# A decoder in one kernel: buffers re-placed in SBUF so that the matmul operands begin at multiples of 128 bytes

## The reference

```python
x = x + _L0_attn_ref(_layernorm(x), ...)            # 32 heads of 16, 8 kv heads, weights sign(w / s)
x = x + _L0_xattn_ref(_layernorm(x), ctx_4096, ...) # 32 heads of 128, 8 kv heads, q and k RMS-normed
x = x + _L0_ffn_ref(_layernorm(x), ...)             # 1792 wide; of each block of 32 only the argmax row is kept
x = x + _L1_attn_ref(_layernorm(x), ...)            # 32 heads of 16, one kv head, ALiBi, causal
x = x + _L1_xattn_ref(_layernorm(x), ctx_4096, ...) # 32 heads of 16, 8 kv heads, mask
x = x + _L1_ffn_ref(_layernorm(x), ...)             # linear plus 2 of 8 LoRA experts, chosen by a gate
```

## Time and profile before

| | |
|---|---|
| median of 3 runs | 2266.28 us (2264.58 to 2267.7) |
| profiled execution, span from first to last instruction | 2260.1 us |
| median less that span | 6.2 us |
| instructions | 39463 |
| PE busy / weight loads busy | 2193.7 us (97%) / 1735.2 us (77%) |
| VectorE, ScalarE, GpSimd busy | 1368.4, 1016.3, 886.8 us |
| DMA queues' share of 16 engines | 10.1% |
| granted TensorE clock, mean | 0.999 of 2.4 GHz |

### The profile page before, as it was taken

How to read it: one execution, slowest core, us unless ns; L and a number is a source line. 1 busy time by engine, 2 the same in 40 slices (tenths; PEclk the granted TensorE clock), 3 DMA queues, 4 the chain that set the end, 5 groups by cost and what they waited for, 6 DMA issues and landing times. The chain is left out here.

```text
span 2260.1 us, 39463 instructions
## 1 busy us (share of the span) xinstructions
PE 2193.7 (97%) x15918; PEld 1735.2 (77%) x15918; DVE 1368.4 (61%) x2383; ACT 1016.3 (45%) x1734; POOL 886.8 (39%) x659
## 2 busy tenths in 40 slices
PE   7997999999999999999999999999999999999998
PEld 4775878778787787877878777888887777777776
DVE  7887533343333453433333458797785888888866
ACT  6774543445435454344543452111102656666532
POOL 2675231432414413143231345121122768777711
PEclk9999999999999999999999999999999999999999
DMA  4000111110112101011010113000002000100001
GB/s 165 2 20 21 57 38 38 38 57 19 38 38 75 57 20 38 38 38 56 20 38 36 38 54 110 0 0 0 0 1 75 20 1 16 49 26 11 2 1 75
DMA packets 23032, 80.65 MB, mean 36 GB/s; under 512 B 4048, under 2 KB 6224, under 8 KB 16720
## 3 DMA queue, kind: packets, MB, share of 16 engines
q1 hardware_dynamic: 22864, 78.28, 10.1%
HBM read 74.08 MB, written 4.19 MB: 35 GB/s over the span
## 5 line engine op out<-in xcount | busy, mean ns | idle before, releaser
L2566 PE MATMUL xat_TP<-shared_rounded 128*128 128x512 f32 x1024 | 322.6, 396 | 5.8 <-issue 5.8
L2240 POOL TENSOR_TENSOR xat_T<-xat_T,xat_mask 128x512 f32<-128x512 f32 x64 | 81.5, 1296 | 523.5 <-DVE xat_T L2330 523.5
L104 PE MATMUL xat_G<-xat_xnT_hi,shared_rounded 128*128 128x512 f32 x768 | 249.1, 397 | 0.0
L2227 POOL TENSOR_TENSOR shared_rounded<-shared_landing,shared_rounded 128x2048 fp32r<-128x2048 f32 x39 | 179.5, 4612 | 153.2 <-ACT shared_rounded L2084 153.2
L2566 PEld LDWEIGHTS xat_TP<-shared_rounded 128*128 128x128 f32 x1024 | 187.2, 188 | 58.0 <-issue 22.4
L2357 DVE TENSOR_TENSOR X<-X,xat_TP 128x512 f32<-128x512 f32 x128 | 87.0, 680 | 198.4 <-PE xat_TP L2566 198.3
L2321 DVE RECIPROCAL xat_q_inv_rms<-xat_OT 128x16 f32<-128x16 f32 x32 | 8.3, 258 | 322.5 <-PE xat_OT L2493 322.5
L2566 PE MATMUL xat_TP<-shared_rounded,xat_oT_lo 128*128 128x512 f32 x512 | 199.8, 390 | 0.0
L104 PE MATMUL ffn_H<-shared_rounded 128*128 128x448 f32 (+1 forms) x816 | 180.1, 369 | 3.3 <-DVE ffn_h_kept L1394 2.0
L1326 POOL TENSOR_TENSOR ffn_one_hot<-ffn_one_hot,ffn_block_rank 128x448 f32<-128x448 f32 x64 | 75.3, 1177 | 254.5 <-DVE ffn_one_hot L1375 254.5
L684 POOL TENSOR_TENSOR two_T<-two_T,two_row_max 128x512 f32<-128x512 f32 x128 | 131.6, 1050 | 102.5 <-DVE two_row_max L775 102.2
(11 more groups left out here) (362 smaller groups left out, 5024.3 us busy)
## 6 DMA issues: line engine op xcount, KB each, us to landing
shared_landing<-in_Cq_q SPq DMA_DIRECT2D x16, 1024.0 KB, 4.9
shared_landing<-in_Cq_o SPq DMA_DIRECT2D x16, 1024.0 KB, 4.9
shared_landing<-in_Cq_kv SPq DMA_DIRECT2D x8, 1024.0 KB, 6.9
shared_landing<-in_ctxT_paired SPq DMA_DIRECT2D x4, 1024.0 KB, 6.8
two_ctxT_raw<-in_ctxT SPq DMA_DIRECT2D x8, 512.0 KB, 3.7
shared_landing<-in_w1T SPq DMA_DIRECT2D x8, 448.0 KB, 3.9
shared_landing<-in_w SPq DMA_DIRECT2D x7, 512.0 KB, 3.5
out<-X SPq DMA_DIRECT2D x6, 512.0 KB, 3.0
```

Of the source, the lines that this page charges most:

```text
L104: last = eng.matmul(out, a, b, start=(n == 0), stop=(n == len(steps) - 1))
L2227: return eng.tensor_tensor(w[1][:, :, :], landed[:, :, :], w[0][:, :, :].bitcast(F32), ALU.subtract)
L2240: eng.tensor_tensor(T[:, n, :, :], T[:, n, :, :], mask[:, :].unsqueeze(1).to_broadcast([P, ROWS, SEQ]), ALU.add)\
L2566: last = eng.matmul(TP[m % 2][:, :], x, w, start=(n == 0), stop=(n == len(steps) - 1))
```

## The change

No instruction is added, removed or moved on any engine, and no wait changes. Only addresses do: of the 18646 instructions of the built program 350 name another buffer or offset for the layer norm's statistics, on ScalarE, VectorE and GpSimd, and none of these is a matmul.

- The layer norm's 6 x 4 raw statistics (96 bytes) leave `ln_small` and become one buffer `stats` behind `ones`, kept for the whole kernel. `headmask_eps` (32 bytes with its padding) and `stats` (96) together are 128, so the shared buffers get phase 0. `ln_small` shrinks from 160 to 64 bytes.
- In every function the large buffers come first, all of sizes that are multiples of 128, and the small ones behind them.
- The cross attention allocates `xnT_hi` and `xnT_lo` itself, ahead of the small buffers.

The phases that follow (address of the buffer in each partition modulo 128, before and now):

| buffer | role | before | now |
|---|---|---|---|
| `shared_rounded`, `shared_rounded2` | nearly all float32r weights, xnT outside the cross attention | 32 | 0 |
| `shared_landing`, `shared_landing2` | landing of the weights' DMAs, staging | 32 | 0 |
| `xat_xnT_hi`, `xat_xnT_lo` | moving operand of the query products | 96 | 0 |
| `xat_qT`, `kT`, `squares`, `V`, `T`, `oT_lo` | cross attention | 32 | 0 |
| `ffn_w2_0`, `ffn_w2_1`, `h_kept`, `hT_lo` | FFN | 32 | 0 |
| `ffn_rT` | FFN | 64 | 0 |
| `gqa_qT`, `Kbd`, `vT`, `Vbd`, `T`, `PT`, `oT_lo`, `xn` | first attention | 64 | 0 |
| `two_Wo0`, `two_Wo1`, `two_o_raw` | second layer | 32 | 0 |
| `two_ctxT_hi`, `two_ctxT_lo`, `two_ctxT_raw` | context of the second layer | 64 | 0 |
| `two_qT`, `Kbd`, `vT`, `Vbd`, `T`, `PT`, `alibi` | second layer | 0 | 0 |
| `ident` | moving operand of transposes | 0 | 0 |

Small buffers keep phases of all four kinds.

```diff
@@ -118,12 +118,12 @@
         ("stat0", "aggr0", "stat1", "aggr1", "inv0", "stat2", "aggr2", "inv1", "stat3", "aggr3", "inv2", "inv3"))}
 
     def __init__(self, mem, X, ident, eps, wrap=0, width=STOK, xn=None, by_tile=False, groups=NST, kept=None, had=False,
-                 small=None):
+                 small=None, stats=None):
         self.X, self.ident, self.eps, self.wrap = X, ident, eps, wrap
-        self.small = mem.sb("ln_small", [P, 10 * ST]) if small is None else small
-        self.stats = self.small[:, 0:6 * ST].rearrange("p (t n) -> p t n", t=ST)
-        self.mv = self.small[:, 6 * ST:8 * ST].rearrange("p (t n) -> p t n", t=ST)
-        self.sd, self.rstd = self.small[:, 8 * ST:9 * ST], self.small[:, 9 * ST:10 * ST]
+        self.small = mem.sb("ln_small", [P, 4 * ST]) if small is None else small
+        self.stats = stats[:, :].rearrange("p (t n) -> p t n", t=ST)
+        self.mv = self.small[:, 0:2 * ST].rearrange("p (t n) -> p t n", t=ST)
+        self.sd, self.rstd = self.small[:, 2 * ST:3 * ST], self.small[:, 3 * ST:4 * ST]
         self.off = 0
         self.other, self.in_other = None, ()
         self.xn = mem.sb("xn", [P, ST, D]) if xn is None else xn
@@ -263,30 +263,33 @@
         Wq, Wk, Wv, rk, rq, rv = (lead[name] for name in ("Wq", "Wk", "Wv", "rk", "rq", "rv"))
         if sign:
             Wo, ro = lead["Wo"], lead["ro"]
-            ln = LayerNorm(mem, X, ident, eps, by_tile=True, groups=NX, kept=lead["xnT"])
+            xn = mem.sb("xn", [P, ST, D])
         else:
             Wo = [mem.sb(f"Wo{n}", [P, KC, D], F32R) for n in range(parts)]
             ro = mem.sb("o_raw", [P, KC, D])
-            ln = LayerNorm(mem, X, ident, eps, groups=NX, xn=lead["xn"], kept=lead["xnT"], had=True)
         if pair:
             cth = mem.sb("ctxT_hi", [P, KC, STOK], F32R)
             ctl = mem.sb("ctxT_lo", [P, KC, STOK], F32R)
             craw = mem.sb("ctxT_raw", [P, 2, STOK])
-            mbias = mem.sb("mask_bias", [P, SEQ])
-            mraw = mem.sb("mask_raw", [P, SEQ], U8)
         qT = mem.sb("qT", [P, 2, KC, STOK])
         Kbd = mem.sb("Kbd", [P, 2, SB, 4, SEQ])
         vT = mem.sb("vT", [P, STOK])
         Vbd = mem.sb("Vbd", [P, 2, SB, 4, 2 * HD])
         T = mem.sb("T", [P, RING, CH, SEQ])
-        mx = mem.sb("row_max", [P, 4, CH])
-        rs = mem.sb("row_sum", [P, 2, 2 * CH])
-        ri = mem.sb("row_inv", [P, 2, 2, CH])
         PT = mem.sb("PT", [P, PTS, 2, 2, P])
         oh = lead["oh"]
         ol = lead["ol"] if pair else mem.sb("oT_lo", [P, 2, KC, P], F32R)
         if pair:
             table = mem.sb("alibi", [P, 2, 2, CH, SEQ])
+        mx = mem.sb("row_max", [P, 4, CH])
+        rs = mem.sb("row_sum", [P, 2, 2 * CH])
+        ri = mem.sb("row_inv", [P, 2, 2, CH])
+        if sign:
+            ln = LayerNorm(mem, X, ident, eps, by_tile=True, groups=NX, xn=xn, kept=lead["xnT"], stats=consts["stats"])
+        else:
+            mbias = mem.sb("mask_bias", [P, SEQ])
+            mraw = mem.sb("mask_raw", [P, SEQ], U8)
+            ln = LayerNorm(mem, X, ident, eps, groups=NX, xn=lead["xn"], kept=lead["xnT"], had=True, stats=consts["stats"])
         if sign:
             scraw = mem.sb("scales_raw", [P, KC + 2])
             scp = mem.sb("scales_mean", [P, KC + 2])
@@ -1168,15 +1171,15 @@
         W1 = lead["W1"]
         W2 = [mem.sb(f"w2_{n}", [P, CHUNKS, D], F32R) for n in range(2)]
         C1, C2, room = lead["C1"], lead["C2"], lead["room"]
+        rT = mem.sb("rT", [P, STOK], F32R)
+        hl = mem.sb("hT_lo", [P, 2, 4 * P], F32R)
+        HM = mem.sb("h_kept", [P, 2, INTER])
+        hh = lead["hh"]
         rank = mem.sb("block_rank", [P, BLK])
-        ln = LayerNorm(mem, X, consts["ident"], consts["eps"], groups=NST + 1, xn=lead["xn"], kept=lead["xnT"], had=True)
-        rT = mem.sb("rT", [P, STOK], F32R)
+        ln = LayerNorm(mem, X, consts["ident"], consts["eps"], groups=NST + 1, xn=lead["xn"], kept=lead["xnT"], had=True, stats=consts["stats"])
         maxes = mem.sb("block_max", [P, 4, QB])
         bmax, zmax = maxes[:, 0:2, :], maxes[:, 2:4, :]
         E1 = mem.sb("one_hot", [P, 3, QB, BLK])
-        HM = mem.sb("h_kept", [P, 2, INTER])
-        hh = lead["hh"]
-        hl = mem.sb("hT_lo", [P, 2, 4 * P], F32R)
         I = [mem.ps(f"I{n}") for n in range(2)]
         H = [mem.ps(f"H{n}") for n in range(2)]
         TP = [mem.ps(f"TP{n}") for n in range(2)]
@@ -1942,6 +1945,7 @@
         V = mem.sb("V", [P, SB, 2 * P])
         T = mem.sb("T", [P, 2 * NU, ROWS, SEQ])
         ol = mem.sb("oT_lo", [P, NH, STOK], F32R)
+        xnT = mem.sb("xnT_hi", [P, KC, HALF], F32R), mem.sb("xnT_lo", [P, KC, HALF], F32R)
         ksum = mem.sb("k_sum", [P, 2 * KV])
         krms = mem.sb("k_rms", [P, 2 * KV])
         kinv = mem.sb("k_inv_rms", [P, 2 * KV])
@@ -1954,7 +1958,7 @@
         norms = mem.sb("norm_weights", [P, 3])
         sel = mem.sb("row_select", [P, QC + NH - 1])
         unused = mem.sb("unused_root", [P, 1])
-        ln = LayerNorm(mem, X, ident, eps, width=HALF, xn=sq)
+        ln = LayerNorm(mem, X, ident, eps, width=HALF, xn=sq, kept=xnT, stats=consts["stats"])
         Kn = T[:, :, :, :].rearrange("p u r s -> p (u r s)").rearrange("p (m d) -> p m d", d=P)
         G = [mem.ps(f"G{n}") for n in range(2)]
         S = [mem.ps(f"S{n}") for n in range(2)]
@@ -2000,7 +2004,7 @@
         y_done, y_added = sig("y_product", 2 * ST), sig("y_added", 2 * ST)
         vec = sig("vector_chain", 2 * U)
         LAST = PASSES - 1
-        nln = LayerNorm(mem, X, ident, eps, xn=lead["xn"], kept=lead["xnT"], groups=1, small=ln.small)
+        nln = LayerNorm(mem, X, ident, eps, xn=lead["xn"], kept=lead["xnT"], groups=1, small=ln.small, stats=consts["stats"])
         NB = [S[0], S[1], S[0], S[1]]
         C1, C2, W1 = lead["C1"], lead["C2"], lead["W1"]
         c1raw, c2raw = lead["c1_raw"], lead["c2_raw"]
@@ -2888,7 +2892,8 @@
 
         X = sb("X", [P, TILES * D])
         ident, few, ones = sb("ident", [P, P]), sb("headmask_eps", [P, 5]), sb("ones", [P, P])
-        consts = {"ident": ident, "headmask": few[:, 0:4], "eps": few[:, 4:5], "ones": ones}
+        stats = sb("stats", [P, 6 * ST])
+        consts = {"ident": ident, "headmask": few[:, 0:4], "eps": few[:, 4:5], "ones": ones, "stats": stats}
         load_constants(nc, signals, X, consts, a)
         with ExitStack() as kept:
             def shared(name, size, dt=F32, stack=kept):
```

## The result

| | before | changed |
|---|---|---|
| median | 2266.99 us (2264.58 to 2267.75, 4 runs) | 2253.83 us (2253.75 to 2255.08, 4 runs) |
| ratio, 95% interval | | 0.9949 (0.9937 to 0.9961) |
| profiled execution, span | 2260.1 us | 2253.3 us |
| its own device time | not listed | 2255.08 us |
| PE busy | 2193.7 us | 2185.9 us |

What follows compares the result with a forecast made beforehand. PE, busy 97% of the span, was taken to bound the kernel. Gains of 10.2 and 1.1 us sum to 11.3, taking the span from 2260.1 to 2248.8 us; adding 6.2 gives 2255, range 2200 to 2270.

Steps and rivals of the forecast that it cites:

- likeliest case: Whole kernel: xnT and ctxT matmuls gain, phases 0/0 cost the same as 32/32; 2247 to 2262 us, chance 0.50.
- fast rival: All float32r matmuls: phase 0 beats other equal phases, so everything gains; about 2207 us, or 2159 at most; chance 0.24.
- No change: Whole kernel: which buffers are read together, not their phase, separates fast from slow streams; 2266 us, chance 0.13.
- slower: Float32r matmuls: phases 0/0 fall into the slow rhythm, +28 us, 2294 us; chance 0.13.
- Part 1: Cross attention's query products: 1536 matmuls with xnT moving go from 233.3 to 226.7 ns, gaining 10.2 us.
- Part 2: Some 210 ctxT matmuls and 64 with gqa_oT_lo gain 4 ns each, 1.1 us together.
- Part 3: All other float32r operands going from 32/32 to 0/0, some 4200 matmuls of 512 columns and 768 of 448: no gain.
- slow rival: Float32r matmuls at 0/0 take the slow rhythm, argued from 448-column matmuls at 206.4 ns; 2294 us, chance 0.13.
- second rhythm: FFN's 448-column stream: equal phases, yet 19.7 ns surplus like unequal pairs' 20.0, so stream length decides with phases.
- Parts 4 to 7: Float32 matmuls, elementwise work, DMA landing buffers and the statistics' buffer: nothing gained or lost.
- The classes "equal" and "unequal" modulo 128: Float32r streams: operands at equal phases cost 226.7 ns per matmul, unequal ones 233, whichever side is off.
- the 6.2 us around the span: Whole kernel: time the runs' median has beyond the profiled span, added to 2248.8 to forecast 2255 us.

Runs made afterwards that it cites:

- e1: Changed kernel with 64 bytes of filler behind the statistics' buffer, putting every large buffer at phase 64; 2255.73 us.
- e4: Changed kernel with 32 bytes of filler behind the statistics' buffer, putting every large buffer at phase 32; 2255.33 us.
- e9: Changed kernel with k_sum and k_rms (128 bytes) moved ahead of the cross attention's xnT, 128 bytes off its weights modulo 256; 2265.00 us.
- e5: Changed kernel with the cross attention's xnT_hi and xnT_lo as slices of one buffer, 16 bytes behind a multiple of 128; 2261.74 us.
- e2: Changed kernel with 32 bytes of filler ahead of the cross attention's xnT_hi, its weights staying at phase 0; 2265.39 us.
- e3: Kernel before, with only the cross attention's xnT_hi and xnT_lo allocated ahead of its small buffers, at their weights' phase 32; 2255.69 us.
- e10: Changed kernel with k_sum, k_rms and q_inv_rms (256 bytes) moved ahead of the cross attention's xnT; 2253.98 us.
- e8: Changed kernel with 32 bytes of filler ahead of rounded2 and ahead of two_Wo0, making some FFN and second-layer pairs unequal; 2256.10 us.
- e11: Changed kernel with the cross attention's oT_lo behind xnT and 32 bytes of filler, every third output product's stationary operand 32 bytes off; 2259.56 us.

## Why the prediction was right, and what in it was not

**Forecast and rivals.** 2255.0 was forecast and 2253.83 measured. The likeliest case came true: the query products to 226.7 (226.9 measured), the output products unmoved. Phase 0 has no worth of its own (e1, e4), so the fast rival falls, and with it the time that the rule of the Trainium skill, "TensorE: Matmul & The Clock Gate", section "Back-to-back issue gap", would give for phase 0: the 13 ns above one column a cycle are still there, at 0/0 too (226.9 measured, 215.8 by the rule). No change and slower fell by the result. "No change" had a true core, though. That the large buffers are at multiples of 128 is indeed no cause (e9 has it and gains nothing), and what the rule of the Trainium skill, "SBUF - State Buffer", section "Specifications (TRN2)", says of 16-byte lines cannot be all: e5 and e2 are whole lines apart and cost 6 and 9 us of the stretch.

**Part 1**, 10.2 us: 9.2 measured in the stretch, as the distances give (9.3). e3 shows that these two lines are worth 10 us, and e2 that without them the rest is not measurable. The medians' 13.2 us are past the sum of 11.3, but at equal granted clock it is 9.5: by that the sum was about 2 us too large. The stretches add up to the same, 9.2 us of the passes and 1.0 of the FFN, which was not forecast, less 0.6 in the second layer (read in e10): part 1 was 1 us too large and part 2 gave nothing. That the medians still came within 2 us is luck as far as the clock made up for it.

**Part 2**, 1.1 us: the distances improved, to 231 ns for ctxT moving and 227 ns for ctxT stationary, 7 matmuls between these two starts of the changed kernel:

```profile
2173.71 0.39 PE L104 MATMUL two_S<-shared_rounded,two_ctxT_lo 128*128 128x512 f32 x1
...
2175.30 0.62 PE L104 MATMUL two_S<-shared_rounded,two_ctxT_hi 128*128 128x512 f32 x2
```

But the second layer did not get shorter: 467.7 us for `two_G` in the kernel before, 468.3 in e10, which has no clock drop there either:

```profile
L104 PE MATMUL two_G<-shared_rounded x564: 386/393/505, 1724.7 to 2193.0; 128*128 128x512 f32 x184, 128*32 128x512 f32 x4
```

168 of the 240 matmuls with ctxT (the prediction had 210 in all) stand in this stretch, so 0.7 us was due there. Pairs that were equal before and after took it back. The mean over 508 distances between matmuls with both operands in `shared_rounded` is 229.2 ns in the kernel before and 230.3 in e10, over the 359 with `two_Wo` 229.8 and 230.9: 1.0 us together. It is no accident of one execution: for the 508, the kernel before, e1, e3 and e8 have 229.1 to 229.4 and the other ten kernels 230.3 to 230.4 (some 10 distances fewer where a clock drop falls among them). What sets these two groups apart, no run shows.

The other half of the part fell flat too. The 91 distances next to a `gqa_oT_lo` operand went from a difference of 224 to 0 and from 231.3 ns to 231.5. Taking 4 of the 6.7 ns for streams of 12 was right for ctxT (4.3), and wrong for `gqa_oT_lo`. So unequal does not cost everywhere; why not there, stays open.

**Part 3**, no change: right for 512 columns in the cross attention, 1.1 ns too low in the second layer, as just said. The 448-column stream of the earlier trace rows is another matter. In the changed kernel, 11 matmuls:

```profile
1462.12 2.38 PE L104 MATMUL ffn_H<-shared_rounded 128*128 128x448 f32 x11
1464.34 0.38 PE L1509 MATMUL ffn_TP<-ident,ffn_h_kept 128*128 128x128 f32 x2
```

2.22 us, 201.8 ns each and not 206.4. But neither piece speaks for its kind: over some 696 distances the mean is 204.7 ns before and 203.5 after (1.2 ns on 768 are 0.9 us). With that falls the argument of the slow rival, which set one piece's surplus of 19.7 ns beside the 20.0 of the unequal pairs: the whole kind has 18.0. So what I called a second rhythm there is no fixed one. The group's first to last start shortened from 361.7 us to 360.7, and to 360.3 and 360.7 in e4 and e10, but in e3 it is 361.6. These pairs are equal in all five. In e8, where 7 of 12 of them are unequal, the mean is 204.7 again, no more than in the kernel before; why, was not tried.

**Parts 4 to 7**, nothing: scores and transposes have the same durations in e1 as in the earlier trace rows (389 and 389, 280 and 276 ns), the DMAs of 1 MB into `shared_landing` land in 4.8 to 6.9 us as before, the normalisation of `gqa_T` takes 1052 ns, as at phase 64, and that of `two_T` 1066:

```profile
L696 POOL TENSOR_TENSOR gqa_T<-gqa_T,gqa_row_inv 128x512 f32<-128x512 f32 x64 | 65.9, 1052 | 56.9 <-DVE gqa_row_inv L802 56.9
L696 POOL TENSOR_TENSOR two_T<-two_T,two_row_inv 128x512 f32<-128x512 f32 x128 | 133.7, 1066 | 13.6 <-DVE two_row_inv L802 13.4
```

**Two more things the number came right in spite of.** The classes "equal" and "unequal" modulo 128 fitted every row that the trace of before had, because its differences were 192, 160 and 96 modulo 256, all slow, and 0. A difference of 64 or 128 was not among them, so the trace could not tell the period nor that unequal is not one price. Had the small buffers been such that xnT came to lie 128 bytes off, the same argument would have predicted a gain that e9 shows is not there; that it lies at 0 modulo 256 in the changed kernel was in the addresses, and I had not looked. And the 6.2 us around the span were not that: the profiled execution of the changed kernel has 2255.08 - 2253.3 = 1.8 us around it, as have the others. So the kernel before's span of 2260.1, at a granted clock of 0.999, very likely belongs to an execution of about 2262, the low end of its runs (2261.7 to 2268.7 over all the comparisons; the three at 0.999 took 2261.7 to 2262.1). The spans therefore differ by less than the medians. Adding the surplus as a constant hid this, and did no harm to the forecast's difference.

## What to carry to other kernels

Where PE is the bound and streams float32r matmuls back to back, print the addresses of the two operands and make their difference a multiple of 256 bytes; here one unequal pair of buffers cost 2.8% of each of its matmuls, and 10 of 2266 us. Expect it in long streams; in pieces of 12 matmuls between other work it was 4.3 ns for one pair of buffers and nothing for another. Alignment of each buffer is neither needed (e1, e4) nor enough (e9). Read the effect as a distance between starts in an unbroken stream, and compare stretches of the same work: it shows in the second digit there, and drowns among clock drops in the span. Take the mean over all distances of a kind before one piece of it is read as a rule, and compare executions at the same granted clock.

## What the runs showed of the hardware that I had not expected

- The distance of the query products, full-rate float32r matmuls, depends on moving less stationary address modulo 256 (226.9 ns at 0, 229.1 at 64, 233.3 at 32; at 128 the passes' stretch is within 1.2 us of that at 32), and not on either address as far as phases 0, 32 and 64 were tried (e1, e4). That it repeats at 256 rests on e10 and on weights that lie 512 bytes apart. Plain float32 matmuls showed nothing of it, and e1. The mechanism behind it stays open: a conflict of the weight load with the moving stream would fit a cost that needs both operands, but no run here shows it. Equal pairs are not all alike either: those of the second layer take 229.1 to 229.4 ns in four of the kernels and 230.3 to 230.4 in the ten others.
- One stationary operand in three off by 32 bytes slows all the matmuls of the stream (233.1 ns, e11).
- After a piece with breaks of about 1 us the granted clock falls to 0.50 for 3.4 us in some executions (changed kernel, 1.40 of 3.40 us busy ahead of it) and stays at 1.00 in others (e10, the same 1.40 of 3.40), though PE is busy again by then; one such drop costs about 1.5 us.
- Equal operands still leave 13 ns above one column a cycle (226.9 against 213.3), and the 448-column products 16 to 18 above their 186.7 (203.1 to 204.7, mean over all). Neither was explained.
